# Flamingo cross-attention with a mixture-of-experts layer: the value projections of each batch are spread over another pair of slots

## What is computed

```python
q = _qdq(x) @ _qdq(wq).T + bq
kv = cond @ wkv.T + bkv                      # cond: (8, 1500, 256)
k, v = jnp.split(kv, 2, axis=-1)
attn = softmax(einsum('bnhd,bmhd->bhnm', q, k) / sqrt(Dh))
o = einsum('bhnm,bmhd->bnhd', attn, v)
out = _qdq(o) @ _qdq(wp).T + bp
x = x + tanh(g_xattn[0]) * out               # then layer norm, router, 16 experts, shared expert
```

## Time and profile before

| | |
|---|---|
| median of 3 runs | 407.97 us (407.75 to 412.41) |
| span of the profiled execution, first to last instruction | 405.0 us |
| median less span, what lies around the instructions | 2.97 us |
| mean granted TensorE clock | 0.951 |
| PE busy | 358.6 us (89%) |
| DVE busy | 303.5 us (75%) |
| ACT busy | 250.9 us (62%) |

### The profile page before, as it was taken

How to read it: one execution, slowest core, us unless ns; L and a number is a source line. 1 busy time by engine, 2 the same in 40 slices (tenths; PEclk the granted TensorE clock), 3 DMA queues, 4 the chain that set the end, 5 groups by cost and what they waited for, 6 DMA issues and landing times.

```text
span 405.0 us, 14019 instructions
## 1 busy us (share of the span) xinstructions
PE 358.6 (89%) x5793; PEld 269.3 (67%) x5793; DVE 303.5 (75%) x656; ACT 250.9 (62%) x412; POOL 124.1 (31%) x116
## 2 busy tenths in 40 slices
PE   0896899999998998998999999998864699999993
PEld 0663468668677766855866776786643587888882
DVE  3888886775776676586577668668896877999993
ACT  3476477777686676776768666567721535666761
POOL 6151462132022122222203300001101054787870
PEclk9999699999999999999999999999985858999998
DMA  7869965565294186166336208544000009635001
GB/s 253 196 157 197 241 146 134 87 159 136 58 171 115 53 152 182 54 106 175 103 61 125 54 14 142 129 137 141 3 2 2 1 1 306 191 116 163 2 0 45
DMA packets 34512, 45.65 MB, mean 113 GB/s; under 512 B 3995, under 2 KB 30299, under 8 KB 34323
## 3 DMA queue, kind: packets, MB, share of 16 engines
q1 hardware_dynamic: 33395, 43.74, 44.5%
q0 software_dynamic: 640, 0.78, 0.9%
q10 hardware_dynamic: 416, 0.26, 0.3%
HBM read 25.08 MB, written 0.47 MB: 63 GB/s over the span
## 4 chain that ended last, share of the span: by engine, by line
PE 76%; DVE 13%; issue 5%; ACT 2%; POOL 2%; DMA 1%; DVEq 0%; ACTq 0%; POOLq 0%
PE PS L1035 35%; PE PS L1101 9%; PE PS L1078 8%; PE PS L1112 7%; PE PS L1363 4%; PE PS L1322 3%; DVE mx L794 2%; PE PS L1088 2%; PE PS L1346 2%; PE PS L1312 1%; DMA x_in<-x 1%; DVE KN L743 1%; PE PS L1279 1%; DVE st L697 1%; DVE mtop L798 1%
## 5 line engine op out<-in xcount | busy, mean ns | idle before, releaser
L794 DVE TENSOR_REDUCE mx<-PS 112x1 f32<-112x500 f32 (+1 forms) x128 | 114.3, 933 | 52.8 <-PE PS L1078 52.7
L501 ACT ACTIVATE PT_all<-PS 128x1344 f32<-128x1344 f32 x64 | 82.6, 1290 | 10.1 <-PE PS L1101 9.9
L1035 PE MATMUL PS<-cT,wkvT 128*128 128x500 f16 x288 | 71.5, 385 | 18.0 <-POOL slot_of L404 11.2
L1035 PE MATMUL PS<-wkvT,cT 128*125 128x256 f16 x576 | 73.2, 279 | 0.0
L1035 PEld LDWEIGHTS PS<-wkvT,cT 128*125 128x125 f16 x576 | 65.3, 139 | 5.3 <-issue 0.5
L395 POOL TENSOR_TENSOR cT<-c_in,cT 128x1000 f16<-128x1000 f32 x18 | 37.5, 2082 | 86.9 <-ACT cT L479 86.9
L1035 PEld LDWEIGHTS PS<-cT,wkvT 128*128 128x128 f16 x288 | 27.5, 99 | 50.8 <-POOL slot_of L404 11.2
L486 ACT ACTIVATE KN<-PS,col_in 128x500 f16<-128x500 f32 x48 | 32.5, 677 | 40.6 <-PE PS L1035 40.6
L1078 PE MATMUL PS<-arena,QC 96*112 96x500 f16 x192 | 52.4, 380 | 3.1 <-issue 2.8
L1101 PE MATMUL PS<-QC,arena 98*128 98x112 f16 x768 | 49.2, 214 | 3.0 <-ACT QC L521 2.9
L493 ACT ACTIVATE V<-PS 125x512 f32<-125x512 f32 x48 | 28.7, 598 | 30.6 <-PE PS L1035 30.6
(11 more groups left out here) (207 smaller groups left out, 463.8 us busy)
## 6 DMA issues: line engine op xcount, KB each, us to landing
arena<-KN SPq DMA_DIRECT2D x144, 125.0 KB, 3.6
c_in<-ctx SPq DMA_DIRECT2D x24, 500.0 KB, 4.5
cT<-W SPq DMA_DIRECT2D x11, 352.0 KB
c_in<-W SPq DMA_DIRECT2D x6, 352.0 KB
cT<-W SPq DMA_DIRECT2D x11, 176.0 KB
arena<-place_far SPq DMA_DIRECT2D x1, 1568.0 KB, 10.0
c_in<-W SPq DMA_DIRECT2D x6, 176.0 KB
PT_all<-L_xattn_wkv SPq DMA_DIRECT2D x1, 512.0 KB, 6.1
```

Of the source, the lines that this page charges most:

```text
L501: act.activation(PT_all[:, u % 4, :].rearrange("p (c k) -> p c k", c=CH), PS[:, 3:6, 0:4 * TP], ACT.Exp, scale=SCORE).then_inc(s["exp_done ...
L794: dve.tensor_reduce(mx[:, u % 2, k:k + 1], PS[0:TP, k:1 + k * (CH - 1), 0:CW], AX.XY, ALU.max).then_inc(s["red_done"], 1)
L1035: ins = mm(out_, w(a, h), x_(b, h), start=first and k == 0, stop=last and k == len(todo) - 1)
```

## The change

The fills of a batch are moved by two slots. The first two slots of a batch now hold that batch's own V3, V4 and V5, and the projections for the next batch (K0 to K5, V0 to V2) start in its third slot. The prologue makes only nine projections for batch 0. The last batch's first two slots, which had no projection, now have V3, V4 (slot 56) and V5 (slot 57); what was done alone in slot 56 (`turn_weights`, the switch to bank 6 for the maxima) moves to slot 58 (`ALONE`). Before, the eight places held (K0,K1) (K2) (K3,V0) (K4) (K5,V1) (V2) (V3,V4) (V5).

```diff
+ALONE = SLOTS - NPAIR + 2
+LATER = 3
 def slot_fills(u):
     b, i = divmod(u, NPAIR)
-    order = ("K0", "K1"), ("K2",), ("K3", "V0"), ("K4",), ("K5", "V1"), ("V2",), ("V3", "V4"), ("V5",)
-    fills = [(name[0], b + 1, int(name[1])) for name in order[i]] if b + 1 < B else []
+    if b >= B:
+        return []
+    order = ("v3", "v4"), ("v5",), ("K0", "K1"), ("K2",), ("K3", "V0"), ("K4",), ("K5", "V1"), ("V2",)
+    fills = [(name[0].upper(), b + name[0].isupper(), int(name[1])) for name in order[i]]
+    fills = [f for f in fills if f[1] < B]
...
-FIRST = ("K0", "V0", "V1", "K1", "V2", "V3", "K2", "V4", "V5", "K3", "K4", "K5")
+FIRST = ("K0", "V0", "V1", "K1", "V2", "K2", "K3", "K4", "K5")
...
-    bank = {... zip(FIRST, (4, 5, 6, 0, 4, 5, 6, 0, 4, 5, 6, 4))}
+    bank = {... zip(FIRST, (4, 5, 6, 0, 4, 5, 6, 4, 5))}
...
 def maxima_bank(u):
-    return 0 if u < SLOTS - NPAIR else 6
+    return 0 if u < ALONE else 6
...
             evacuate_values(0, 2)
             context_hi(1, 0)
-            evacuate_values(0, 3)
             keys_hi(0, 2)
             context_hi(1, 1)
-            evacuate_values(0, 4)
-            evacuate_values(0, 5)
             keys_hi(0, 3)
...
-                early = u > SLOTS - NPAIR
+                early = u > ALONE
...
-                if u == SLOTS - NPAIR:
+                if u == ALONE:
                     turn_weights()
...
-            project_values(0, 3)
             project_keys(0, 2)
-            project_values(0, 4)
-            project_values(0, 5)
             project_keys(0, 3)
...
-            need(pe, "v_done", 5)
+            need(pe, "kl_done", 2)
```

More of the change, by code:

```diff
@@ L62, in slot_fills @@
     return fills
-FIRST = ("K0", "V0", "V1", "K1", "V2", "V3", "K2", "V4", "V5", "K3", "K4", "K5")
+FIRST = ("K0", "V0", "V1", "K1", "V2", "K2", "K3", "K4", "K5")
 def bank_uses():
-    bank = {(name[0], 0, int(name[1])): b for name, b in zip(FIRST, (4, 5, 6, 0, 4, 5, 6, 0, 4, 5, 6, 4))}
+    bank = {(name[0], 0, int(name[1])): b for name, b in zip(FIRST, (4, 5, 6, 0, 4, 5, 6, 4, 5))}
     for u in range(SLOTS + 2):
@@ L1069, in scores @@
                 b, i = divmod(u, NPAIR)
-                need(pe, "aug_done", min(u - 1, SLOTS - NPAIR))
+                need(pe, "aug_done", min(u - 1, ALONE))
                 if i % 4 == 0:
@@ L1095, in turned_scores @@
                     pe.wait_ge(s["consts"], NCONST)
-                    need(pe, "v_done", 6)
+                    need(pe, "v_done", 6 - LATER)
                     need(pe, "kl_done", 6)
@@ L1159, in pe_slot @@
                 fills = slot_fills(u)
-                if u == SLOTS - NPAIR + 1:
+                if u == ALONE + 1:
                     pe.wait_ge(s["act_weights"], 2)
-                early = u > SLOTS - NPAIR
+                early = u > ALONE
                 if u < SLOTS:
```

## The result

| | before | after |
|---|---|---|
| median | 410.19 us, 4 runs (407.75 to 412.42) | 416.69 us, 4 runs (414.81 to 418.89) |
| profiled execution: span | 405.0 us | 413.3 us (its time 415.09) |
| mean granted TensorE clock | 0.951 | 0.948 |

The account below looks back on a forecast made before the run. PE was taken as the bound in most stages (76% of the chain), DVE's chain in the prologue. Minus 4.1 (front), plus 3.5 (end), zero for pauses: minus 0.6 on 405.0, span 404.4, plus 2.97: 407.4 us; range 403.0 to 410.8.

Parts of the forecast that it names:

- Prologue: Start to slot 0: PE idle 4.3 us, then clock low 4.6 us; scores of slot 0 at 36.2 against 34.44.
- rival (a): Prologue: the clock stays up, 2.2 us less than the forecast, 405.2 us; chance 0.18.
- First slots: Slots 0 to 2: low-half wait goes, they take 3.4, 3.8 and 4.0; slot 3 at 47.4, 3.4 us earlier.
- as the pair of 8.10 they give 0.7 more: Slots 3 and 4: 8.82 us before, expected to take 8.10 like slots 54 and 55, so 0.7 us won.
- GpSimd's steps follow the same slots as before. I cost all this at nothing: Loop: moved fills, evacuations, DMAs and GpSimd's steps cost zero unless a DMA is late by over ten microseconds.
- the front as a whole: Start through slot 4: 4.1 us earlier in all, 3.4 up to slot 3 and 0.7 in slots 3 and 4.
- rival (d): Front gains nothing as DVE, or batch 2's context for ACT, is late; end costs 3.5 us: 411.5; chance 0.12.
- DVE's wait at 46.22: Slot 2 in the trace of before: DVE's reduction waited for PE, taken as a sign that DVE is not late.
- The count: Instructions ahead of place 4: 48 lower, so pauses come 48 instructions later, then reach scores or K5 of place 6.
- I take the same 5.8 us: Loop pauses of PE, one a batch: sum unchanged at 5.8 us, bounded by zero and 11.4 us.
- Rival (c): Loop: pauses become seven of 1.63 us, at K5's first matmul, the worst place: plus 5.6, 413.0; chance 0.08.
- The end: Slots 56 to 59: 13.4 us against 9.94, 3.5 us more; only 0.7 of three projections' 4.2 us is hidden.

Follow-up runs that it names:

- one_input_warm: Changed kernel with DVE's two small steps in one-operand form, plus 16 unused matmuls in PE's idle time of the prologue: 1.030, 421.75 us.
- count32_before: Kernel before, with 64 already-met waits (32 instructions) put ahead of the tokens' turn in the prologue: 1.039, 424.27 us.
- mtop_reduce_after: Changed kernel with DVE's small maximum made by a reduction over one operand in place of a two-operand step: 1.011, 415.25 us.
- x1_late_after: Changed kernel with GpSimd's two steps on row_in and x1 moved behind its batch loop: 1.013, 414.42 us.
- pool_gaps_after: Changed kernel with GpSimd waiting for its own last operation after each query product and low half, which leaves short gaps: 0.997, 411.34 us.
- after_again: The changed kernel measured again, unaltered, beside three others on the same chip: 1.019 against the kernel before, 415.6 us.

## Why the prediction was wrong

**Prologue: right in kind, slot 0 forecast 2.1 late.** The idle time before the tokens is 3.65 (4.3 forecast). The clock falls behind it, though only at about 29.0 and not when PE starts again (28 to 29 has 1.00, 29 to 30 has 0.50), and it stays low for 3.4 us (4.6 forecast); tokens to scores take 6.06 against 4.38, 1.7 more (2.2 forecast). The tokens came at 28.07 and not 29.65: 0.90 of that was there already at the first queries' product (20.76 for 21.66), and the rest lies in DVE's chain, where one step took 0.56 in place of 1.17. Taking the fall away altogether (one_input_warm) won 1.3 us, not the 2.2 that told rival (a) from the forecast.

**First slots: right up to slot 4.** The wait for the context's low half is gone, the clock is full from 41 to 48, and slots 0 to 2 take 11.04 (11.2 forecast). Slot 3 is 5.63 ahead, 2.2 more than forecast.

**The step that failed** is the sentence on slots 3 and 4, "as the pair of 8.10 they give 0.7 more", with "GpSimd's steps follow the same slots as before. I cost all this at nothing". They took 15.40. DVE was not late by its load; one step of it was shut out for 5.70 us. The term for slots 3 and 4 came out at +6.58 in place of -0.7, which is 7.28 of the 8.9 us between the forecast's -0.6 and the 8.3 of the spans. The earlier slots gave 2.23 back, so the front as a whole came out at +0.95 in place of -4.1, 5.05 off. That is rival (d), the front gains nothing because DVE is late, with another reason than it gave (one step shut out by GpSimd): it named load and DMA, and argued against itself with DVE's wait at 46.22. It also put its price at 411.5, since it took the front at zero and the pauses at no change.

Why after has this and before not is seen in the traces but was not tested: in after GpSimd's two low halves of the context follow its query products without a gap, since ACT's high half was there (49.29) before GpSimd asked for it; in before ACT's came at 55.44, and GpSimd's gap of 0.53 let DVE in. It takes no change of the fills to lose that gap: count32_before had none, and a DVE step of 5.63 at 51.58.

The Trainium skill has the rule in "SBUF — State Buffer" (Who interferes with whom): a DVE instruction with two inputs in SBUF contends with a GpSimd instruction that reads SBUF, one with at most one such input, outside its two-port modes, does not. The experiments agree on both halves (5.70 and 5.31 against 0.15 to 0.22). The page adds (Summary: rules for kernel authors) that the one that comes second waits until the first finishes; here it waited over the four touching operations that were left, 5.70 us, of which none takes over 2.1, so for the length the measurement decides.

**The pauses: the place right, the sum wrong.** The count was nearly right (48 lower; the compiled list has 51 at the scores of place 4 and 63 at those of place 6), and place 6 was right. "I take the same 5.8 us" was not: the five in the loop are 8.2, and the sixth falls in slot 60, outside any fill. Loop and slot 60 cost 3.74 more than the zero that the sum held. Rival (c) had the mechanism, and its size (seven of 1.63, 11.4 in all) is nearer the 10.2 measured than the forecast's 5.8. Its statement that the first matmul of K5 was the worst place is wrong: after itself has 2.47 in the scores, and count32_before shows 2.85 and 2.40 in the turned scores.

The Trainium skill says in "Runtime: NRT & Kernel Launch" (Instruction fetch mechanics) that instructions come in blocks of 256 and that crossing one is mostly hidden. The period of 256 is in every trace here; at most crossings nothing shows, as the page says, but up to ten of them in a loop cost 0.4 to 3.2 us each, and there are 21 us between two kernels that differ by 32 instructions of no work. That the pause is the fetch itself is inferred from period and place; no run measured a fetch.

**The end: right.** Slots 56 to 59 took 13.02 (13.4 forecast), slot 57 waits 0.83 for the augment (1.2 forecast), 3.08 more than before.

The terms together, as errors of the forecast: front 5.05, pauses 3.74, end -0.42, the rest 0.53, which makes the 8.9.

**What the change is worth.** With DVE's steps mended, the two kernels cannot be told apart, without padding (0.995 and 0.998) nor with it (0.982 and 0.984). Without padding the front is 3.80 ahead at slot 4 and the end gives 3.0 back, so stall and pauses apart the change is worth some 0.8 us, close to the 0.6 of the forecast's sum. That closeness is in part luck: both kernels begin slot 0 at 33.5, where the forecast had the change 1.8 later, and the whole 3.80 is won in slots 0 to 2. Open stays which disturbance falls on a front for a given count: one_input_warm had a slot 5 of 7.24 us, with a pause of 3.00 in it, though its DVE was free.

## What to carry to other kernels

Look in the trace for small steps of an engine whose duration is many times their usual, even if nobody waits for them yet: two such rows of before (2.20 and 1.47 for 0.16) were the warning, and moving work earlier made one of them the bound. Read the time that a change gains at every slot up to the end, not as a difference of the totals, since a stall can eat a gain in one slot. And when two long unrolled kernels are compared, try each at another count of instructions before a few per cent are put down to the change, and look whether the padding itself is hidden in both.

## What the runs showed of the hardware beyond expectation

A DVE step on 112 numbers with two operands in SBUF can wait through a whole row of GpSimd's operations: 5.70, 5.63, 5.31 and 4.26 us in after, count32_before, mtop_reduce_after and x1_late_after, each ending 0.02 or 0.03 us after the last of the touching operations. A gap of 0.08 us is enough: pool_gaps_after, with GpSimd just as busy, has no step over 1.94. One boundary without a gap let DVE in too (51.14 in before, behind GpSimd's sum).

TensorE's pauses lie 256 instructions apart, or a multiple of that. Of instructions without work ahead of the loop, 32 took the kernel before from 1 to 1.039 (with a stall of DVE in it) and after from 1.016 to 1.033; 64 took the two with one-operand steps from 0.998 to 0.984 and from 0.995 to 0.982.

A fall of the granted clock to half follows some pauses and not others of the same length: it came after the 2.47 at 200.71 in after_again, and not after the 2.47 at 200.45 in after.
